# Two macaron feed-forward layers with attention: where the second layer's shared expert of batches 5 to 7 is computed

## The reference, cut to what matters

```python
x = x + 0.5 * ffn(layernorm(x))
x = x + attention(layernorm(x))
x = x + 0.5 * ffn(layernorm(x))
# ffn(x): y + z per token
#   scores = softmax(x @ gate_w.T); of 4 groups of 4 experts two groups are kept, of these 2 experts chosen
#   y = sum over the two chosen experts e of weight_e * ((silu(x @ We1[e] + be1[e]) * (x @ We3[e] + be3[e])) @ We2[e] + be2[e])
#   z = silu(x @ ws1 + bs1) * (x @ ws3 + bs3) @ ws2 + bs2        # the shared expert, for every token
```

## Time and profile before

| | us |
|---|---|
| median of 3 runs | 1550.31 (1538.19 to 1560.65) |
| the profiled execution's own time | 1541.71 |
| its span, first to last instruction | 1540.0 |
| layer 2: routing stage | about 890 to 1183 |
| layer 2: experts stage | 1183 to 1469 |
| layer 2: held parts and final sums | 1469 to 1540 |

### The profile page before, as it was taken

The page is one execution under the profiler, slowest core; times in us unless marked ns, Lnnn a source line. Parts: engine busy times, 40 slices in busy tenths (PEclk is TensorE's granted clock), DMA queues, the critical chain, the costliest instruction groups (busy, mean ns, idle before and its releaser), DMA issues.

```text
span 1540.0 us, 27583 instructions
## 1 busy us (share of the span) xinstructions
PE 1273.1 (83%) x7304; PEld 991.1 (64%) x7304; DVE 917.9 (60%) x3386; ACT 678.9 (44%) x1474; POOL 575.2 (37%) x593
## 2 busy tenths in 40 slices
PE   5999777799879995999999989779777998898840
PEld 3656444587767784888888866446444887787720
DVE  5767534465556665777767656566453665555565
ACT  4444410366556662333343454434212766565500
POOL 2576454255445450000000004736542554454410
PEclk9999888899999998999999999889888999999975
DMA  9422115344434434111210001212133544444379
GB/s 383 138 88 88 59 70 114 121 144 140 121 118 134 121 103 123 55 58 60 61 57 27 1 0 57 91 49 84 69 104 100 151 146 132 122 138 119 93 285 370
DMA packets 93324, 173.08 MB, mean 112 GB/s; under 512 B 17496, under 2 KB 60525, under 8 KB 91891
## 3 DMA queue, kind: packets, MB, share of 16 engines
q1 hardware_dynamic: 63606, 93.25, 20.6%
q0 software_dynamic: 26112, 67.82, 12.5%
q10 hardware_dynamic: 3456, 10.25, 1.7%
HBM read 88.64 MB, written 86.79 MB: 114 GB/s over the span
## 4 chain that ended last, share of the span: by engine, by line
PE 64%; DVE 10%; another core or an unknown queue 7%; ACT 7%; issue 7%; DMA 3%; POOL 1%; DVEq 0%; ACTq 0%; POOLq 0%
PE bank L544 17%; PE bank L425 9%; PE bank L554 8%; PE bank L442 6%; PE bank L535 5%; PE bank L588 4%; PE bank L577 4%; PE bank L651 3%; DMA w<-routed_rows 3%; PE bank L407 2%; PE bank L556 2%; PE bank L397 2%; ACT xn L808 1%; ACT rows L713 1%
## 5 line engine op out<-in xcount | busy, mean ns | idle before, releaser
L1332 POOL DMA_INDIRECT routed_rows<-xn,rdest x288 | 283.6, 985 | 326.3 <-DVE rw L1145 208.5
L544 PE MATMUL bank<-rows 128*128 128x128 f32 x2304 | 310.2, 278 | 19.1 <-ACT rows L796 12.6
L544 PEld LDWEIGHTS bank<-rows 128*128 128x128 f32 x2304 | 280.5, 192 | 30.9 <-ACT rows L796 22.9
L1310 POOL DMA_INDIRECT expert_rows<-rows,slots x192 | 186.2, 970 | 187.0 <-DVE slots L959 113.3
L1156 DVE SCALAR_TENSOR_TENSOR rows<-bank,tile_b,rows 128x128 f32<-128x128 f32 x288 | 101.0, 351 | 225.3 <-ACT rows L801 170.6
L554 PE MATMUL bank<-w,rows 128*128 x576 | 177.5, 390 | 46.1 <-DVE rows L1156 45.8
L442 PE MATMUL bank<-ws,work 128*128 128x256 f32 x512 | 154.8, 432 | 68.9 <-DVE work L1085 30.0
L796 ACT COPY rows<-w 128x512 f32 x288 | 178.5, 620 | 15.7 <-issue 9.4
L442 PEld LDWEIGHTS bank<-ws,work 128*128 128x128 f32 x512 | 99.3, 213 | 103.3 <-DVE work L1085 33.8
L795 ACT COPY rows<-bank 128x256 f32<-128x256 f32 x288 | 106.7, 370 | 112.8 <-PE bank L535 101.8
L801 ACT ACTIVATE rows<-bank,tile_b 128x128 f32<-128x128 f32 x288 | 104.9, 364 | 81.4 <-PE bank L544 77.1
(11 more groups left out here) (184 smaller groups left out, 2155.2 us busy)
## 6 DMA issues: line engine op xcount, KB each, us to landing
rows<-expert_rows SPq DMA_DIRECT2D x288, 130.5 KB
rows<-routed_rows SPq DMA_DIRECT2D x32, 512.0 KB, 4.8
w<-routed_rows SPq DMA_DIRECT2D x10, 1024.0 KB, 19.1
out<-xres ACTq DMA_DIRECT2D x16, 512.0 KB, 7.0
xres<-in_x SPq DMA_DIRECT2D x7, 1024.0 KB, 7.7
expert_rows<-pad SPq DMA_DIRECT2D x48, 130.5 KB
rows<-routed_rows SPq DMA_DIRECT2D x6, 1024.0 KB, 16.0
routed_rows<-xn,rdest POOLq DMA_INDIRECT x288
```

The costliest lines, as they stand in the source:

```text
L544: last = nc.tensor.matmul(rh_ps[t % 2][:, n * P:(n + 1) * P], m.rw13[:, t % 2, c * C + n * INTER:c * C + (n + 1) * INTER], m.rT[:, t % 2, ...
L1310: nc.gpsimd.indirect_dma_start(out=d.xg, out_offset=bass.IndirectOffsetOnAxis(ap=m.slots[:, b % XS, k, i:i + 1], axis=0), in_=xs[:, i, :], ...
L1332: nc.gpsimd.indirect_dma_start(out=d.yt, out_offset=bass.IndirectOffsetOnAxis(ap=m.rdest[:, n:n + 1], axis=0), in_=m.ry[:, n, :], in_offse ...
```

## The change

In the second layer all parts of the shared expert of batches 5, 6 and 7 are held (12 ups and 6 downs in place of 1 and 2); TensorE runs them one after another behind the experts, and ScalarE and VectorE take them between the pieces of the final sums, three parts for two pieces. In the routing stage the held parts are left out, while what lay between their matmuls (gates, transposes, the steps of `route_work`) stays. The first layer's order is the same. `ry` moves from `xn` to `att`, since `xn` now holds batch 6's transposed tokens until the end.

```diff
-    m.ry = m.xn
+    m.ry = m.att[:, 0:SLOTS * C].rearrange("p (n c) -> p n c", n=SLOTS)
...
-HELD = range(45, PARTS)
+HELD = (tuple(range(45, PARTS)), (29,) + tuple(range(31, PARTS)))
...
+def early(L, kind):
+    return sum(part_of(n)[0] < BATCHES and part_of(n)[1] == kind for n in range(PARTS) if n not in HELD[L])
+def first_held(L, kind):
+    return next((b, k) for b, of, k in map(part_of, HELD[L]) if of == kind)
+def beside(n):
+    each = 3
+    return HELD[1][each * n // 2:each * (n + 1) // 2]
...
-                if r % BATCHES == BATCHES - 1 and u == 3:
+                if (r % BATCHES, u) == first_held(r // BATCHES, "up"):
                     pe.wait_ge(s.rgated_ready, TILES * (r // BATCHES + 1))
...
-                if r % BATCHES == BATCHES - 1 and g == 0:
+                if (r % BATCHES, g) == first_held(r // BATCHES, "down"):
                     pe.wait_ge(s.ry_scaled, TILES * (r // BATCHES + 1))
...
-            def shared(L, n, between=lambda j: None):
+            def shared(L, n, between=lambda j: None, held=False):
                 b, kind, k = part_of(n)
-                if b == BATCHES:
+                if b == BATCHES or (n in HELD[L]) != held:
+                    for j in range(4):
+                        between(j)
                     return
...
-                pe.wait_ge(s.gated_ready, 4 * (BATCHES * L + 7) + 3)
-                pe.wait_ge(s.y_added, NT * (BATCHES * L + 7))
+                pe.wait_ge(s.gated_ready, 4 * BATCHES * L + early(L, "up"))
+                pe.wait_ge(s.y_added, NT * BATCHES * L + 4 * early(L, "down"))
...
             experts(1)      # ScalarE
-            for n in HELD:
-                shared(1, n)
-
             ov = d.out.rearrange("b (p j) c -> b p (j c)", p=P)
-            for n in range(BATCHES * PIECES):
-                b, h = divmod(n, PIECES)
-                act.wait_ge(s.f_added, 2 * n + 2)
-                act.dma_start(ov[b][:, h * PIECE:(h + 1) * PIECE], piece(n)).then_inc(s.f_stored, 16)
+            for n in range(BATCHES * PIECES + 1):
+                for k in beside(n):
+                    shared(1, k, held=True)
+                if n:
+                    b, h = divmod(n - 1, PIECES)
+                    act.wait_ge(s.f_added, 2 * n)
+                    act.dma_start(ov[b][:, h * PIECE:(h + 1) * PIECE], piece(n - 1)).then_inc(s.f_stored, 16)
...
             experts(1)      # VectorE
-            for n in HELD:
-                shared(1, n, iter(()), 0)
-
             for n in range(BATCHES * PIECES):
+                for k in beside(n):
+                    shared(1, k, iter(()), 0, held=True)
+                if n == PIECES * 5:
+                    assert 3 * (n + 1) // 2 <= len(HELD[1])
                 x, y = piece(n), m.yf[n % FSLOTS]
```

More of the change, by code:

```diff
@@ L661, in _ @@
             experts(0)
-            for n in HELD:
-                shared(0, n)
+            for n in HELD[0]:
+                shared(0, n, held=True)
             pe.wait_ge(s.att_weights_in, 16 * len(att_loads))
@@ L697, in _ @@
             experts(1)
-            for n in HELD:
-                shared(1, n)
+            for n in HELD[1]:
+                shared(1, n, held=True)
         @block.scalar
@@ L729, in copy_xT, with shared @@
                 nc.scalar.copy(m.xnTs[r % BATCHES % XS][:, c, g * HALF:(g + 1) * HALF], xT_ps[:]).then_inc(s.xT_copied, 1)
-            def shared(L, n):
+            def shared(L, n, held=False):
                 b, kind, u = part_of(n)
-                if b == BATCHES or kind == "down":
+                if b == BATCHES or kind == "down" or (n in HELD[L]) != held:
                     return
@@ L1091, in add_shared, with shared @@
                 nc.vector.scalar_tensor_tensor(x, y_ps[i % 2][:, 0:C], 0.5, x, ALU.mult, ALU.add).then_inc(s.y_added, 1)
-            def shared(L, n, work, steps):
+            def shared(L, n, work, steps, held=False):
                 b, kind, k = part_of(n)
                 r = L * BATCHES + b
-                if b == BATCHES or kind == "up":
+                there = b < BATCHES and (n in HELD[L]) == held
+                if not there or kind == "up":
                     for _ in range(steps):
                         next(work, None)
-                    if b < BATCHES:
+                    if there:
                         gated(r, k)
@@ L1240, in _ @@
             experts(0)
-            for n in HELD:
-                shared(0, n, iter(()), 0)
+            for n in HELD[0]:
+                shared(0, n, iter(()), 0, held=True)
             for h in range(PAIRS):
```

## The result

The kernel after the change takes 1556.66 us (median of 20 runs, 1539.42 to 1572.21), the kernel before beside it 1549.57 us (median of 20, 1525.0 to 1575.65). The ratio is 1.0107, with an interval of 1.0065 to 1.0149: about 1% slower. This ratio counts only the executions within 1.5% of the fastest of their kernel, and as the times of one kernel spread over 3% here, it differs from the ratio of the two medians, 1.0046. The forecast was 0.7% faster. The time lies in the range, on the wrong side of the kernel before. The profiled execution took 1554.38 us.

The account below looks back on a forecast made before the run. TensorE (83% busy) was taken to bound the kernel, with GpSimd gaps in routing and DMA limiting the final sums. Terms -34 + 3 + 20 = -11 us gave 1530.7 profiled, 1539 as median; range 1522 to 1562.

Parts of the forecast that it names:

- The scatters: Layer two's routing: batch 6's scatter starts at 1102, batch 7's at about 1123, ending at 1143.5 in place of 1165.3.
- the sum of the two parts: Batch 6's turn: two up parts removed, 2.5 us on VectorE and 4.3 on TensorE, 6.8 us; scatter could start at 1104.
- The tail: Behind batch 7's scatter: first load after 2.9 us, rows 2.7 later, pads free; first transpose at 1149, not 1182.88.
- Half clock at the experts' start: First expert tiles: TensorE, almost idle from about 1107 to 1149, starts at half clock; costs 3 us, between 0 and 6.
- The final stage: Final sums: a piece on VectorE stalls each down part, 12.5 us per pattern; 90.7 us in all, 19.7 more.
- The sum's sign: Whole kernel: -34 + 3 + 20 = -11 us, so faster, by 0.7%.
- the routing gain: Layer two's routing stage: 34 us saved until TensorE's first transpose, less 3 us for half clock.
- Rival 2: Routing stage: late signals keep both GpSimd gaps, only the wait behind the last scatter is won; +11, 1561 us; chance 0.20.
- Rivals 1 and 3: Final stage: additions find VectorE free, only 7.5 us added, 1527, chance 0.15; or half clock, +48, 1598, chance 0.05.

Follow-up runs that it names:

- The split of the pads: Eight of layer two's 16 pads issued by ScalarE's queue, on top of pieces only right behind the down parts: 1574.97 us, ratio 0.992.
- pieces only right behind the down parts: Changed kernel, but VectorE takes final-sum pieces only after a down part's four additions: 1566.36 us, ratio 0.9919; run again 1578.15 us, 0.9959.

## Why the prediction was wrong

In us, from the stages of the traces: "late signals" is the first trace of the change against the earlier trace rows and their trace, "quiet" the change on the quiet chip against the kernel with only `ry` moved there:

| step | forecast | late signals | quiet |
|---|---|---|---|
| scatters of batches 5 to 7 | -21.8 | -19.6 | -6.7 |
| last scatter to the experts' first send | -9.2 | -1.4 | -0.5 |
| final stage | +19.7 | +22.2 | +20.5 |
| sum | -11 | +1 | +13.3 |

- **The scatters**: the step held on the chip for which it was made. GpSimd became the bound for batch 7 as forecast, and batch 6's scatter came 27.2 us after batch 5's where I had 23.9 (1102 - 1078.13), or 25.9 by the sum of the two parts (1104). Its *reading* was wrong all the same. I put the gaps of the earlier trace rows down to the shared expert, 6.8 us of it by two rows. On a quiet chip the same shared expert leaves gaps of 2.9 and 3.1 us. Most of the 12.8 us was lateness, not the parts' own time. It went with the parts where signals are late, and isn't there to be saved where they aren't.
- **The tail is the step that failed.** I had 5.6 us from the last scatter to the first transpose "as before", and the pads at nothing: the tables "are made meanwhile, since they need only batch 7's row numbers, and the 16 pads too". The pads' cover was a gap: in the earlier trace rows they start 0.4 us after the scatter of batch 7 does, right behind 12.86 us of idle GpSimd. Without the gap the first eight come 2 to 5 us apart, they end after the scatters, and the first load waits for a pad's landing. It is 13.8 us (1157.2 to 1170.97) instead of 5.6, and 8.2 of the forecast's gain of 11 is gone. The split of the pads shows this by experiment: 6.1 us of it come back. On a quiet chip the tail is 4.8 us (1031.5 to 1036.26), but there it was short before as well: TensorE's last held-over part ended at 1037.7 and the transpose stood at 1038.73, 7.1 us after the scatter's end and not 17.6.
- **Half clock at the experts' start** was right in kind and near in size: 8.5 us from the first transpose to the first send in place of 6.2, +2.3 (forecast 3). The granted clock was 0.51 from 1102 to 1178, so 1.2 GHz for nearly all of it, and 1.00 from 1178 to 1190.
- **The final stage**: its mechanism and size were right, 12.66 us per pattern for 12.5 and +20.5 on a quiet chip for +19.7. By the forecast's own count, from TensorE's first held matmul, it is 71.4 to 92.7 there, +21.3. In all traces of the change the first down part waits 3.5 to 3.6 us behind piece 0; in the two with late signals it then runs its first groups at half clock (2.08 for four records), which costs 1.3 us more than in the quiet one, where 1.13 stands behind the same wait. VectorE's order is about half of this price, 10.5 of 22.2 us, and it works both ways: the stage is 81.5 with the pieces behind the down parts, 114.4 with two ahead of them. The other half, 81.5 against 70, stays when the order no longer holds TensorE up.
- **The sum's sign** hung on the routing gain being above 20. It was 21.0 where signals are late and 7.2 where they aren't. Rival 2 gave +11 and 1561 by "the gaps stay and the tail is won"; its price came out near the median, 1556.66, by luck, since its mechanism did not: the gaps went and the tail stayed. Rivals 1 and 3 are refuted for the change itself, by 92.0 of final stage and by the 1.13 us behind each of the repeated waits.
- **What stays open**: by the stages of single traces the change costs +1 us where signals are late, by the medians +7.1 (1556.66 - 1549.57) and +11.5 (1555.2 - 1543.71), by the ratios 1.1 and 1.8%. Stages that the change doesn't touch differ between executions by more than that: layer one's experts took 278.9 us in the first trace of before, 282.3 and 291.5 in the two of after, and from the first scatter to batch 5's of layer two it is 1029.8 and 1046.9 us in two traces of the kernel before, 1034.0 and 1038.6 in the two of after. I can't say from these traces whether the change moves some of that lateness into other stages or whether it is chance. Nor is it known what makes signals late.

No version beats the kernel before by much. The best measured are "pieces only right behind the down parts" (0.9919 and 0.9959) and the same with split pads (0.992), about 0.4 to 0.8% on chips with late signals. On a quiet chip they weren't run; by the stages the first would be about -7.2 + 11.3 (81.5 - 70.2) = +4 us there, an estimate.

## What to carry to other kernels

Work that is moved beside a second stream is paid in good part by the order in one in-order engine's queue, which busy shares don't show: put each long item of the other stream right behind the last thing the busy engine waits for, and here 10 of 22 us come back. Before a gap is booked as a gain, ask which small DMAs live in it; here 16 pads that had cost nothing took 31 us once the gap was gone, where signals are late, and held the next stage's first load. And a gap in one profiled execution is not always the work's own: the idle times whose releaser is "remote" may not be there on the next chip, and a change priced on them needs a second trace. Two traces are compared by stages, since their spans also hold a start that differs by 5 to 10 us by chance.

## What the runs showed of the hardware

- **The same kernel takes 1362 us on one occasion and 1544 to 1584 us on others**, whatever the kernel: chip 3 on one occasion, chips 9 (two occasions) and 12 on the others. Of the 182 us between the two traces of the kernel after, TensorE's busy time accounts for 51 (1280.3 and 1229.5); the rest is waiting. The experts' stages are 236 against 274 to 307 us each, and the waits marked "remote", summed over all of a trace, are none in four traces against 162 to 230 us in eleven. Late waits reach 21.1 us (VectorE for the gate's logits).
- **DMA issues on SyncE's queue take 2 to 5 us each while GpSimd sends scatters back to back** where signals are late (16 in 30.75 us, of which the last eight are 0.5 apart, from 4.5 us after the last scatter's recorded end on), mostly 0.5 to 0.6 us on a quiet chip beside the same scatters (16 in 8.87). Where the pads begin right behind a gap of GpSimd they take 9.6 to 11.7 us in all. ScalarE's queue is as slow at the same time (4.2 us per issue), so spreading the pads over both brings only half of the tail back; breaks in the scatters don't bring it back.
- **Half clock came back with each wait of 4.0 to 5.1 us in a pattern of 17.5 us, and with none of 1.6 us in one of 12.7**: rows of 1.84 to 2.08 and of 1.03 to 1.13 us for the same four records. In between it goes either way: behind one wait of 3.5 to 3.6 us, ahead of the first down part, the row is 2.08 in two traces of the change and 1.13 in the third.
- **The first 50 us of one and the same kernel take two lengths**: the same two records of 512 columns at 24 to 26 us into the span take 1.10 us in some executions and 2.06 in others, and the first scatter starts 5 to 10 us later.
